# Three PSUM banks for the gate and up products, and a VectorE that takes each unit one slot later

## What is computed

```python
def nvfp4_linear(x, w, s_in):
    s_w = fp4_global_scale(w)
    xq = fake_quant_nvfp4(x, s_in)
    wq = fake_quant_nvfp4(w, s_w)
    return jnp.einsum('bsh,oh->bso', xq, wq)
gate_out = nvfp4_linear(x, gate_w, s_in[0])          # 512 -> 2048
up_out = nvfp4_linear(x, up_w, s_in[0])              # 512 -> 2048
hidden = jax.nn.silu(gate_out) * up_out
return nvfp4_linear(hidden, down_w, s_in_down[0])    # 2048 -> 512
x = x + jnp.tanh(g_ffn[1]) * ...                     # this block's result
```

## Time and profile before

| | us |
|---|---|
| median of three runs (lowest, highest) | 1818.28 (1814.18, 1821.37) |
| the profiled execution: device time | 1823.66 |
| its span in the profile | 1821.9 |
| TensorE matmul busy | 1371.2 (75%) |
| VectorE busy | 1421.6 (78%) |
| ScalarE busy | 692.5 (38%) |
| GpSimd busy | 243.9 (13%) |

### The profile page before, as it was taken

How to read it: one execution, slowest core, us unless ns; L and a number is a source line. 1 busy time by engine, 2 the same in 40 slices (tenths; PEclk the granted TensorE clock), 3 DMA queues, 4 the chain that set the end, 5 groups by cost and what they waited for, 6 DMA issues and landing times.

```text
span 1821.9 us, 24307 instructions
## 1 busy us (share of the span) xinstructions
PE 1371.2 (75%) x8120; PEld 705.4 (39%) x8120; DVE 1421.6 (78%) x2437; ACT 692.5 (38%) x2105; POOL 243.9 (13%) x197
## 2 busy tenths in 40 slices
PE   5044737799787978698778978797869886988663
PEld 4021315344453436344543345343634453434321
DVE  6988896878787687787787878768777778786695
ACT  2112206451455227441644146422734164425310
POOL 1102200131003200230013100320013001310000
PEclk9556868899889989999999989998999999999888
DMA  9175761042101420233004210142023300420012
GB/s 348 68 243 146 188 143 36 6 88 64 42 1 35 93 59 14 35 62 77 25 7 87 58 48 1 35 93 59 14 35 65 75 24 6 87 58 24 7 24 51
DMA packets 267433, 120.08 MB, mean 66 GB/s; under 512 B 244090, under 2 KB 244602, under 8 KB 265750
## 3 DMA queue, kind: packets, MB, share of 16 engines
q1 hardware_dynamic: 267286, 118.27, 26.5%
HBM read 49.04 MB, written 8.39 MB: 32 GB/s over the span
## 4 chain that ended last, share of the span: by engine, by line
issue 43%; DVE 26%; PE 18%; DMA 4%; SPq 4%; ACT 3%; POOL 2%; POOLq 0%; DVEq 0%; ACTq 0%
PE bank L1075 13%; PE bank L1164 5%; DVE amax L826 2%; DVE pair L835 2%; DVE hid L831 2%; SPq L314 2%; DVE th L868 2%; SPq L303 1%; DVE pair L850 1%; DMA region<-region 1%; ACT region L535 1%; DVE pair L843 1%; DMA hqt<-pair 1%; DVE sc L797 1%; DVE stats L686 1%
## 5 line engine op out<-in xcount | busy, mean ns | idle before, releaser
L1164 PE MATMUL bank<-w_dn,region 128*128 128x512 fp8e4 x1024 | 243.7, 386 | 40.0 <-DMA region<-region 40.0
L1075 PE MATMUL bank<-w_up,xt 128*128 128x512 fp8e4 x1024 | 248.6, 391 | 32.7 <-ACT region L499 17.4
L1075 PE MATMUL bank<-w_gate,xqt 128*128 128x512 bf16 x512 | 147.9, 416 | 122.2 <-DVE th L868 78.4
L508 ACT ACTIVATE th<-bank,half_cg 128x512 f32<-128x512 f32 x128 | 88.0, 687 | 350.2 <-PE bank L1075 350.2
L426 POOL TENSOR_TENSOR region<-g,region 128x512 f16<-128x512 f32 x128 | 178.9, 1402 | 300.9 <-ACT region L499 292.9
L868 DVE SCALAR_TENSOR_TENSOR th<-th,bank 128x512 f32<-128x512 f32 x128 | 87.6, 684 | 138.4 <-ACT th L508 138.3
L535 ACT ACTIVATE region<-bank,nm 128x77 f32<-128x77 f32 x512 | 160.0, 345 | 68.2 <-DVE nm L914 68.2
L1075 PE MATMUL bank<-w_down,hqt 128*128 128x512 bf16 x512 | 134.3, 422 | 56.9 <-DMA hqt<-pair 56.9
L496 ACT ACTIVATE g<-bank 128x512 f32<-128x512 f32 x128 | 76.4, 597 | 247.2 <-PE bank L1075 188.2
L1164 PEld LDWEIGHTS bank<-w_dn,region 128*128 128x128 f16 x1024 | 101.0, 99 | 167.4 <-issue 52.0
L1075 PEld LDWEIGHTS bank<-w_up,xt 128*128 128x128 f16 x1024 | 102.0, 101 | 163.5 <-issue 55.4
(11 more groups left out here) (206 smaller groups left out, 2473.6 us busy)
## 6 DMA issues: line engine op xcount, KB each, us to landing
xin<-in_x SPq DMA_DIRECT2D x16, 512.0 KB, 4.1
out_x<-x SPq DMA_DIRECT2D x16, 512.0 KB, 3.0
region<-in_w_up_t SPq DMA_DIRECT2D x1, 4096.0 KB, 12.9
hid<-in_gate_w SPq DMA_DIRECT2D x4, 1024.0 KB, 5.2
x<-in_gate_w SPq DMA_DIRECT2D x4, 1024.0 KB, 6.1
hid<-in_up_w SPq DMA_DIRECT2D x4, 1024.0 KB, 5.2
x<-in_up_w SPq DMA_DIRECT2D x4, 1024.0 KB, 5.8
hid<-in_down_w SPq DMA_DIRECT2D x4, 1024.0 KB, 4.9
```

The source lines that it names most:

```text
L508: eng.activation(th[:, u % 2, :], bank[4][:, :], ACT.Tanh, scale=half_cg[:, :]).then_inc(sg["th"], 1)
L1075: last = mm(out, lhs, rhs, start=(n == 0), stop=(n == len(pairs) - 1))
L1164: last = mm(bank[2 + t % 2][:, :], ht[i][:, t % 2, f, :], w_dn[:, f, :], start=(f == 0 and i == 0), stop=(f == KF - 1 and i == 1))
```

## The change

Product number 2u (gate) and 2u+1 (up) go to bank 4 + (number modulo 3). Unit u's gate product now waits for `hid` of unit u-2, its up product for `hg` of unit u-1. For unit 1, whose gate product is the first to land in bank 6, TensorE also waits until the attention's last reader of that bank is done. In phase B VectorE does `hidden(u)` in the slot after the one in which TensorE makes unit u, and both halves of `quant4` stand one slot later: for the four tiles in slots 7/8, 14/15, 21/22 and 28/29. `POST_AT`, which places `down4` on TensorE and `out4` on VectorE, keeps its slots. In the tail only the banks and the waits are new.

```diff
-QUANT_AT = {TILE_AT[t] + 4 + i: (t, q) for t in range(TILES) for i, q in enumerate(((0, 1, 2), (3, 4)))}
+QUANT_AT = {TILE_AT[t] + 5 + i: (t, q) for t in range(TILES) for i, q in enumerate(((0, 1, 2), (3, 4)))}
...
+        def gu_bank(u, i):
+
+            return 4 + (2 * u + i) % 3
...
-                eng.activation(th[:, u % 2, :], bank[4][:, :], ACT.Tanh, scale=half_cg[:, :]).then_inc(sg["th"], 1)
+                eng.activation(th[:, u % 2, :], bank[gu_bank(u, 0)][:, :], ACT.Tanh, scale=half_cg[:, :]).then_inc(sg["th"], 1)
...
-                        if s in GU_AT:
-                            hidden(s4, GU_AT[s])
+                        if s - 1 in GU_AT:
+                            hidden(s4, GU_AT[s - 1])
                         if s in QUANT_AT:
...
-                for i, (w, read) in enumerate(((w_gate, "hg"), (w_gup, "hid"))):
-                    if u:
-                        want(pe, read, g, u)
+                for i, w in enumerate((w_gate, w_gup)):
+                    if i == 0 and u >= 2:
+                        want(pe, "hid", g, u - 1)
+                    if i == 1 and u:
+                        want(pe, "hg", g, u)
...
+                    if u == 1 and i == 0:
+                        want(pe, "p3l", g)
-                    last = product(bank[4 + i][:, :], [(xqt[:, t, k, :], w[:, k, ns]) for k in range(KD)])
+                    last = product(bank[gu_bank(u, i)][:, :], [(xqt[:, t, k, :], w[:, k, ns]) for k in range(KD)])
```

More of the change, by code:

```diff
@@ L867, in hidden @@
                 want(dve, "th", g, u + 1)
-                eng.scalar_tensor_tensor(th[:, u % 2, :], th[:, u % 2, :], 1.0, bank[4][:, :], ALU.add,
+                eng.scalar_tensor_tensor(th[:, u % 2, :], th[:, u % 2, :], 1.0, bank[gu_bank(u, 0)][:, :], ALU.add,
                                          ALU.mult).then_inc(sg["hg"], 1)
@@ L871, in hidden @@
                 want(dve, "gu", g, u + 1)
-                eng.tensor_tensor(buf[:, n * D:(n + 1) * D], th[:, u % 2, :], bank[5][:, :], ALU.mult).then_inc(sg["hid"], 1)
+                eng.tensor_tensor(buf[:, n * D:(n + 1) * D], th[:, u % 2, :], bank[gu_bank(u, 1)][:, :], ALU.mult).then_inc(sg["hid"], 1)
             def quant4(g, t, parts, buf=hid):
```

## The result

The changed kernel takes 1888.05 us (median of four runs, 1885.02 to 1902.04) against 1817.03 us (four runs, 1814.18 to 1821.37): 1.0405 times the time before, 95% interval 1.0358 to 1.0453. The profiled execution took 1902.04 us, the longest of the four, so its span of 1900.2 us lies 78.3 us above the profiled span before, where the medians lie 71 us apart.

What follows compares the result with a forecast made beforehand. It took VectorE's chain to tile 3's hq, which holds up down4 at each phase B end, as the bound; + 67.4 - 3.0 - 1.7 = + 62.7 us on the median 1818.28 gave 1881.0 us, range 1867 to 1898.

Steps and rivals of the forecast that it cites:

- the last slots: End of phase B: tile 3's hq comes later behind newly preceding VectorE work, 10.5 us at six boundaries, 4.35 at the seventh.
- The bound: End of phase B: down4 of tile 3 has no slack, so any delay of its hq moves the next phase A equally.
- The query: First query after the transposes of slot 26: 0.5 us later, as unit 14 now stands behind the four x_lo.
- The third bank in the middle of phase B: Stalls at units 1 and 5: gate product runs ahead, gaining 0.2 us in seven periods and 0.4 in four, 3.0 us together.
- The tail: In the tail, VectorE's wait ahead of a hidden goes, with shorter ones beside it: gain 1.7 us, between nothing and 4.
- The clock at the boundaries: At down4 of tile 3, longer TensorE idleness costs nothing more through the low clock; upper end 1 us a boundary.
- The first one: Rotation works and phase A absorbs the late hq: all 78.4 us of gate waits won would give 1740 us; chance 4%.
- The second one: Gains and losses cancel, the boundary loss being under 2 us each: about 1820 us; chance 3%.
- the third: Last slots: only the 7.41 us of moved work counts and ql0 brings no wait, + 41 us, 1859; chance 8%.
- The fourth: Worse than the sum: low clock paid in full, third bank's gains lost, ql0 waits up to 1 us more: 1898; chance 13%.

## Why the prediction was right, point by point

Predicted were 1881 us (1867 to 1898) and a loss by the last slots; measured were 1888.

**The bound.** That `down4` of tile 3 ends phase B without slack held: each microsecond taken from or put ahead of `hq` came out at TensorE's wait one for one, 6.17 for 6.15 with `norm1` behind, 2.95 for 2.98 with the `ql` behind, 6.16 for 6.15 with `norm1` ahead in the kernel before.

**The last slots.** Predicted 10.0 us between first query and `hq` (10.5 less the query's own 0.5). The rows give 907.42 - 883.64 = 23.78 us after and 872.01 - 858.22 = 13.79 before: 9.99. Of it TensorE saw 9.4, since it could start 4.4 us after the end of the second half where it had taken 5.0 (911.84 - 907.42 and 877.05 - 872.01). I had counted nothing for that. At the seventh, predicted 3.85, measured 3.79. The wait for the first `ql` was 2.98 us; I had worked out 3.0.

**The query.** Predicted 0.9 us earlier at the transposes and 0.5 later at the query, a loss of 1.4 in between; measured 1.0. TensorE's wait for `hg` of unit 14 is there, ahead of the up product of unit 15:
```profile
882.76 1.04 PE L1079 MATMUL bank<-w_gup,xqt 128*128 128x512 bf16 x4 [1.15 <-DVE th L872]
```
But the 0.9 us ahead of the transposes were not there to be lost (next point), so from the first gate product to the query a period lost 1.4 us where I had counted 0.5. This and the sooner landing offset each other: the 67.4 us of the last slots came out as 61 + 7 = 68, closer than the two parts were.

**The third bank in the middle of phase B.** This is a term that was mis-sized: predicted a gain of 1.3 us a period, measured a loss of 0.4 to 0.6. The waits did move as said (at unit 1, 3.18 us ahead of the up product where 3.40 had stood ahead of the gate product). What I left out is the clock behind them. The fourth period, before and after:
```profile
960.36 1.04 PE L1075 MATMUL bank<-w_gate,xqt 128*128 128x512 bf16 x4 [3.40 <-DVE th L868]
961.24 1.03 PE L1075 MATMUL bank<-w_gup,xqt 128*128 128x512 bf16 x4
962.10 1.89 PE L1075 MATMUL bank<-w_up,xt 128*128 128x512 fp8e4 x8
```
```profile
996.16 1.04 PE L1079 MATMUL bank<-w_gup,xqt 128*128 128x512 bf16 x4 [3.18 <-DVE th L872]
997.03 3.45 PE L1079 MATMUL bank<-w_up,xt 128*128 128x512 fp8e4 x8
```
The eight matmuls behind the wait take 1.56 us more; the windows view gives a granted clock of 1.00 for 960 to 964 us before and 0.65 for 996 to 1000 us after. They take 3.3 to 3.6 us in six of the seven periods after, and 1.89 in all seven before. Over the whole stretch TensorE's matmuls were busy 1.2 us a period longer (88.9 against 87.7), for the same matmuls, and it idled 0.8 less, where I had expected 1.3 less. So the clock is the larger part of the miss and the smaller saving the rest. Seven periods of some 1.8 us are 12 us, most of the difference between the predicted 62.7 us and the measured ratio's 74.

**The tail.** The other mis-sized term: predicted - 1.7, measured + 1.9 to + 2.4. The lower clock behind it is measured, and two experiments, banks alone and banks with a tail on two, show that it comes with the third bank.

**The clock at the boundaries.** Nothing was predicted, and nothing is there: after 14.2 us of idleness the 16 matmuls took 5.3 to 6.4 us where they had taken 5.1 to 6.3 after 4.9. I looked for the clock at the longest gap, where it was lost already, and not at the short ones that the change moves.

**The rivals.** The first one fell with the wait of 14.2 us: phase A absorbed nothing. Its premise, a gain of up to 78 us, fell too: with the banks alone the run is 4 us faster. The second one (less than 2 us a boundary) fell with the 9.4 us, the third (no wait for `ql0`) with the 2.98 us. The fourth had two things right that my sum had not: the third bank's gains were lost, and the clock cost time, but at another place than the boundary.

## What to carry to other kernels

When a step is moved by a slot, write out what the engine does in the slots that it passes, at the last occurrence above all: here one table entry put a 6 us layer norm of the next group and a wait for another engine ahead of the one result that all engines wait for. A further PSUM bank lets a product run ahead by one; it does not shorten the work of the engine that holds the bank, so count one product a stall, not the stall. Then look what TensorE runs right behind a wait that is moved: its clock can fall there and cost more than the product gained, as it did behind unit 1 (1.56 us against a product of 0.87).

## What I had not expected of the hardware

TensorE's granted clock does not follow from the amount of idleness alone. In the tail, from the second tile's first wait to the first `down4`, TensorE of the kernel before idled 4.83, 2.05, 0.64 and 1.84 us, with eight products in between, and ran that `down4` at a clock of 1.00. With three banks it idled 4.82, 0.88, 0.56 and 2.79 us, with seven (one gate product had moved ahead of the first wait), 9.1 us in all against 9.4, and ran it at 0.55, about the lower of its two levels (1.2 GHz against 2.4). It repeats in every kernel with three banks in the tail and is gone with two. What exactly the chip looks at these runs don't tell.
